# An eight-period pipelined kernel (Mamba, MoE, LSTM attention, MoE) on one core: TensorE gets matmuls whose result nobody reads in slots that hold no wide one

## What is computed

```python
x = layernorm(x + mamba(x))          # conv, 16 states a channel, a linear scan over time
x = layernorm(x + moe16(x))          # 16 experts, top 2, and one shared expert
x = layernorm(x + lstm_attention(x)) # LSTM of width 20, then a Gaussian position attention
x = layernorm(x + moe4(x))           # 4 layers of 4 experts, top 2

def step(carry, xg_t):               # the LSTM, 1024 steps one after the other
    h, c = carry
    i, f, gg, o = split(xg_t + h @ W_hh.T, 4)
    c = sigmoid(f) * c + sigmoid(i) * tanh(gg)
    h = sigmoid(o) * tanh(c)
```

## Time and profile before

| | |
|---|---|
| median of 3 runs | 3135.28 us (3131.15 to 3146.74) |
| the profiled execution | 3143.73 us |
| its span, first to last instruction | 3141.7 us |
| mean granted TensorE clock | 0.803 |
| first period (LSTM steps 0 to 127) | 327.6 to 646.2 us |
| attention slots 4 to `att` of periods 1 to 7 | 312 us together |
| LSTM's last step | ends at 2934.8 us |

### The profile page before, as it was taken

One profiled execution on the slowest core, in us unless ns is written; L12 is line 12 of the kernel. 1 busy time (PEld: TensorE's weight loads), 2 busy tenths in 40 slices (PEclk: granted clock), 3 DMA queues, 4 the chain that ended last, 5 costly groups with the idle time before them and its releaser, 6 DMA issues.

```text
span 3141.7 us, 30770 instructions
## 1 busy us (share of the span) xinstructions
PE 2537.0 (81%) x7208; PEld 1271.2 (40%) x7208; DVE 1943.4 (62%) x6569; ACT 1386.7 (44%) x4620; POOL 1062.8 (34%) x913
## 2 busy tenths in 40 slices
PE   4776884479996989789886998788978997889598
PEld 1122443244444444344444443444444444444344
DVE  4857587357775777567766677577766555444422
ACT  3232433435544555445544554445534444444233
POOL 4735257104542445235432455244422001100200
PEclk7587655659996899878996899789978996788699
DMA  3231332003321233113220332122311220111021
GB/s 108 68 84 54 89 99 72 25 13 100 101 66 28 80 96 90 42 46 101 78 71 27 92 97 75 25 73 84 92 33 46 65 64 21 34 64 58 10 81 57
DMA packets 111774, 204.70 MB, mean 65 GB/s; under 512 B 14799, under 2 KB 24422, under 8 KB 111592
## 3 DMA queue, kind: packets, MB, share of 16 engines
q1 hardware_dynamic: 111592, 202.75, 22.1%
HBM read 195.36 MB, written 7.34 MB: 65 GB/s over the span
## 4 chain that ended last, share of the span: by engine, by line
PE 41%; DVE 28%; ACT 14%; issue 7%; POOL 1%; DVEq 0%; POOLq 0%; ACTq 0%
PE p_hid L656 8%; DVE state L1197 7%; PE p_turn L905 7%; PE p_misc L666 4%; ACT cell_t L919 4%; DVE cell L935 3%; DVE add_c L932 3%; PE p_acc L666 3%; DVE weighed L1206 2%; DVE p_turn L929 2%; PE p_misc L354 2%; PE p_gate L465 2%; DVE hist L940 2%; PE p_turn L475 1%; ACT cand L916 1%
## 5 line engine op out<-in xcount | busy, mean ns | idle before, releaser
L905 PEld LDWEIGHTS p_turn<-hist,w_hh 22*128 22x128 f32 x2048 | 371.6, 225 | 1148.2 <-DVE hist L940 1013.9
L905 PE MATMUL p_turn<-hist,w_hh 22*128 22x4 f32 x2048 | 457.3, 291 | 420.2 <-DVE hist L940 402.2
L656 PE MATMUL p_hid<-xhat,w 128*128 128x512 f32 x1024 | 581.8, 652 | 1.1 <-ACT hid L714 0.7
L919 ACT ACTIVATE cell_t<-cell 20x4 f32<-20x4 f32 x1024 | 207.7, 203 | 701.7 <-DVE cell L935 701.7
L1135 POOL TENSOR_TENSOR drive<-du,rows 128x512 f32<-128x512 f32 x256 | 473.4, 1849 | 63.2 <-DVE state L1197 44.9
L929 DVE SCALAR_TENSOR_TENSOR p_turn<-p_turn,cell 20x4 f32<-20x4 f32 x1024 | 170.7, 167 | 500.8 <-ACT p_turn L915 478.9
L714 ACT ACTIVATE hid<-p_hid,b1f 128x512 f32<-128x512 f32 x512 | 351.6, 687 | 243.1 <-PE p_misc L666 151.1
L388 POOL TENSOR_TENSOR n_rstd<-n_var,minus_half 128x4 f32<-128x4 f32 x56 | 62.0, 1108 | 1098.3 <-DVE n_var L376 1098.3
L1197 DVE TENSOR_TENSOR_SCAN state<-decay,drive 128x512 f32<-128x512 f32 x256 | 398.1, 1555 | 25.2 <-POOL drive L1139 15.7
L1154 POOL TENSOR_TENSOR y<-y,weighed 128x512 f32<-128x512 f32 x192 | 242.4, 1262 | 450.5 <-DVE weighed L1206 449.9
L940 DVE SCALAR_TENSOR_TENSOR hist<-p_turn,cell_t 20x4 f32<-20x4 f32 x1024 | 162.7, 159 | 275.6 <-ACT cell_t L919 275.6
(11 more groups left out here) (204 smaller groups left out, 3161.5 us busy)
## 6 DMA issues: line engine op xcount, KB each, us to landing
rows<-rows_dram SPq DMA_DIRECT2D x128, 512.0 KB, 5.0
w<-w_dram SPq DMA_DIRECT2D x128, 256.0 KB, 2.7
w<-in_w2T SPq DMA_DIRECT2D x128, 256.0 KB, 2.7
comb_b<-comb_dram SPq DMA_DIRECT2D x64, 512.0 KB, 4.7
rows<-comb_dram SPq DMA_DIRECT2D x128, 128.0 KB, 2.9
w<-in_w1T SPq DMA_DIRECT2D x16, 256.0 KB, 2.8
w_dram<-w SPq DMA_DIRECT2D x16, 256.0 KB, 2.4
out_xT<-result SPq DMA_DIRECT2D x8, 256.0 KB, 2.5
```

Source lines behind the costliest of these rows:

```text
L656: nc.tensor.matmul(p_hid[:, v % 2, :], w1[:, v // FB, (v % FB) * P:(v % FB + 1) * P], xhat[:, :], start=True, stop=True).then_inc(g_h, 1)
L905: nc.tensor.matmul(gate_bank(i)[:, :, t:t + 1], w_hh[:, :], before, start=False, stop=False, skip_group_check=True).then_inc(gates_done, 1)
L919: nc.scalar.activation(cell_t[64:64 + PE_, :], cell[32:32 + PE_, :], ACT.Tanh, scale=0.5).then_inc(cell_tanh, 1)
```

## The change

A function `fill_pe` multiplies `mean_w` (a constant 128x128 matrix) with columns of `w_gate` (expert weights that lie in SBUF) into a PSUM bank that holds nothing at that time. `filling` decides for each slot of the periods 0 to 7 whether one is issued, how wide (512 columns, or 256 where `layer0` has a wide matmul in that slot) and into which bank. It is called on TensorE's program alone, last in the slot:

```diff
+    def fill_pe(bank, columns):
+        nc.tensor.matmul(bank[:, 0:columns], mean_w[:, :], w_gate[:, 0:FB, :].rearrange("p u c -> p (u c)")[:, 0:columns],
+                         start=True, stop=True)
+
+    L0_WIDE = {1, 5, 7, 49, 51} | set(range(11, 46))
+
+    def filling(i, slot, o, k0, with0, pre_done, has_pre):
+        wide0 = 1 if with0 and k0 in L0_WIDE else 0
+        if i == 0:
+            if pre_done == 0 or pre_done > 10:
+                return p_hid[:, 1, :], CT >> wide0
+            return None, 0
+        q = i - 1
+        att, tail = att_slots(q), att_slots(q) + L * LAYER
+        if 4 <= slot < att:
+            wide1 = 1 if 8 <= slot < 8 + q or slot == 10 + q else 0
+            bank = p_acc1 if slot < 8 else p_hid[:, 1, :]
+            return (bank, CT >> wide0) if not wide1 else (None, 0)
+        if slot >= tail + 5 and (pre_done > 10 or not has_pre):
+            return p_hid[:, 1, :], CT
+        return None, 0
...
-            if layer0 and not (heavy and slot < CH) and slot >= (L0_AT if layer1 else 0):
+            with0 = bool(layer0) and not (heavy and slot < CH) and slot >= (L0_AT if layer1 else 0)
+            if with0:
                 next(layer0, None)
+                k0 += 1
...
+            if fill and slot < CH and i < NCH:
+                bank, columns = filling(i, slot, o, k0 - 1, with0, done["pre"], u + 1 < NCH)
+                if columns:
+                    fill(bank, columns)
```

More of the change, by code:

```diff
@@ L1428, in period @@
         slot = 0
+        fill, k0 = of.get("fill"), 0
         def advance(g, what, n):
@@ L1573, in start @@
                 pe.wait_ge(prep_v, 3)
-            of = dict(pre=mamba_pre_pe, scan=mamba_scan_pe, leave=mamba_leave_pe, fold=fold_pe, layer0=layer0_pe, layer1=layer1_pe, lstm=lstm_pe)
+            of = dict(pre=mamba_pre_pe, scan=mamba_scan_pe, leave=mamba_leave_pe, fold=fold_pe, layer0=layer0_pe, layer1=layer1_pe, lstm=lstm_pe,
+                      fill=fill_pe)
             whole(dict(of, start=start))
```

## The result

| | before | after |
|---|---|---|
| median of the timed runs | 3135.22 us (3131.15 to 3146.74) | 3159.77 us (3158.19 to 3161.61) |
| the profiled execution | 3143.73 us | 3161.61 us |
| its span | 3141.7 us | 3158.6 us |
| mean granted TensorE clock | 0.803 | 0.852 |

What follows compares the result with a forecast made beforehand. No one engine was taken to bound the kernel; the LSTM step chain sets the pace. Gains of 21, 20, 8 and 4 sum to 53 us, less 5 for clock falls: 48 off the 3135.28 us median, 3087 us, range 3060 to 3112.

Steps and rivals of the forecast that it cites:

- rival A: Whole kernel slower because the fills run at the low clock: about 3236 us; chance 0.08.
- Price of a cold fill in a bare step: Low-clock slot with nothing else in the way: a fill makes 1.83 us into about 2.4, 0.55 lost.
- First period, -21 us: First period: 55 bare steps give 10 us, expert matmuls 7, late starts 4, preparing 1.5, less 1.5 for the cold start.
- The folding (-7): First period, 383.4 to 481.8 us: expert matmul steps shorten from 4.0 to 2.6 us at full clock; 7 us gained.
- term 1: The first period's 21 us gain; called wrong if the folding's steps keep their length while the clock is full.
- Attention, -20 us: Attention, seven stretches: bare steps give 8 us, late starts 16, shorter L905 3, less 7 for cold starts and collisions.
- rival B: No change: VectorE's scans and attention's element-wise chain set the steps, collisions take two per period, 15 us; 3126 us; chance 0.12.
- The layers' first slots, -8: First slots of the layers start at full speed: about 4 us in the first period with layers, 1 in the others.
- Ends, -4 net: Periods' ends: 31 bare steps give 5.5 us, less three cold starts of 0.55; 4 us net gained.
- Slots 0 to 3, 0: Start of each period, not filled: L590's 22-row matmuls stay at clock 0.50, so nothing counted for 28 steps.
- C: The clock flickers, at full speed for two thirds of the filled time: half of the gain, 3112 us; chance 0.12.
- D: More gain than forecast: late starts go nearly whole and faster preparation lets scans begin sooner; 3055 us; chance 0.10.

Runs made afterwards that it cites:

- e7_clear: Changed kernel without the 35 fills in slots of L347, L456, L612 or L1284 (224 fills left): 3125.04 us, ratio 0.9965 to the kernel before.
- e4_rows22: Changed kernel with all 259 fills multiplying 22 rows in place of 128, same columns: 3261.7 us, ratio 1.0363 to the kernel before.
- e5_early: Changed kernel with each fill directly behind the slot's LSTM matmul, not last in the slot (255 fills): 3141.37 us, ratio 1.0022 to the kernel before.
- e8_chosen: Changed kernel cut to 56 fills: first period from slot 97 (two in slot 97) and ends of the last three periods; 3131.43 us, ratio 0.9988.
- e11_single: The kernel of e8_chosen with one fill in slot 97 instead of two, all else equal: 3132.93 us in its one run.
- the parts: Three kernels, each with only the changed kernel's fills of the first period, attention or periods' ends: ratios 1.0019, 0.9973 and 0.9980 to the kernel before.
- e10_combined_early: Changed kernel with 152 fills directly behind the LSTM matmul: first period from slot 97, attention without L347, L456, L612, fewer at ends; 3123.36 us, 0.9954.

## Why the prediction was wrong

**The step that failed** is "So I expect full speed after the first two or three slots of a filled stretch, and 0.9 or more in it". The filled stretches show 0.69, 0.75, 0.75 and 0.88 in the first period, 0.64 to 0.85 in attention, 0.73 to 0.89 at the ends. "Two or three slots" was only somewhat short: after a wait the clock was full again within three filled steps in the folding (376.71 to 387.29) and after five behind slot 97 (602.27 to 614.80). What failed is that it stays full. Of the eleven waits of TensorE of more than 2 us in the filled stretches, nine (both of 3.3 us, and seven of the nine of 2.2 to 2.8) began at the full clock and ended at the low one, so the steps behind them are cold. The prediction took 5 us off for this. The runs show 98 of 258 filled steps (38%) low in both kernels, at 0.40 us each, 39 us, against a gain of 16 in the 158 full ones: a smaller form of rival A. The prediction's own break-even ("at half of the filled time gain and loss are about even") does not follow from its own prices: at 0.55 lost and 0.18 gained, three in four must be warm, and three fifths were.

Step by step:

- *Bounds and chain.* Right: the step is 1.83 us at the low clock and 1.62 at the full one, 0.2 us won (0.18 said).
- *Price of a cold fill in a bare step.* 0.55 said, 0.69 measured (2.52 us). The fill starts 0.5 us after L905, as said, but the next L905 follows 2.01 us behind its start (602.78 to 604.79), not the 1.86 of the earlier trace rows.
- *First period, -21 us.* It came as +9.4. The bare steps were right where the clock held: 1.62 us from slot 103 on. They were counted too high, though: by the trace of the kernel before, 45 steps of the first period and 21 of attention last 1.78 to 1.87 us, where the prediction has 55 and 46. The folding (-7) was wrong in its second half: steps of 2.70 at the full clock came as worked out (2.6), but those that begin after a wait last 5.08 where 4.0 stood before, and the rest did not shorten: without the fills behind L1284, at a clock of 0.77, the stretch takes 98.2 us, and 98.4 before. That was named in the prediction as the sign that term 1 is wrong.
- *Attention, -20 us.* It came as +7.2. The gain from late starts is there where the clock is full: in period 1 the step of L606 and L447 took 4.0 us from L905 to L905 and takes 2.2 (the first rows below); from L606's start, as in the earlier trace rows, it is 3.5 and 1.9. But one collision per period at 0.7 was too few and too cheap: the step behind L347 alone costs 1.2 to 1.9 us in each of periods 2 to 6, from `hist` to `hist`, 8.6 us together, more than the whole loss of attention; with the fill left out there it is gone (`e7_clear`: 2.05 us in period 3). Attention as a whole still took 2.8 us more than before in `e7_clear`, at its other fills. This was in part rival B's collision, in size about its 15 us.

```profile
678.03 0.38 PE L905 MATMUL p_turn<-hist,w_hh 22*128 22x4 f32 x2
...
680.23 0.38 PE L905 MATMUL p_turn<-hist,w_hh 22*128 22x4 f32 x2
```

```profile
687.85 0.60 PE L456 MATMUL p_up<-ident,comb 128*16 128x128 f32 x4 [1.27 <-DVE comb L428]
688.29 1.02 PE L1410 MATMUL p_hid<-w_gate,mean_w 128*128 128x512 f32 x2
689.25 0.38 PE L905 MATMUL p_turn<-hist,w_hh 22*128 22x4 f32 x2
```

The second of these is the collision that the prediction took from the earlier trace rows: L905 0.96 us behind the fill's start, as said.
- *The layers' first slots, -8.* -1.5 in the layers' stretches as a whole, and +5.9 in the last norm; the layers move by more than this from build to build, so the term can't be told.
- *Ends, -4 net.* +3.5: where the clock held, steps of 1.62 (before 1.83), but five of the seven ends start cold and the other two fall to the low clock after their first fill.
- *Slots 0 to 3, 0.* Nearly right: 70.7 to 67.9 us. Above all in periods 1, 6 and 7 part of them ran at the full clock (means of 0.75, 0.73 and 0.60), which the prediction had not foreseen; the fills behind them all start at the low one, as it said.
- *The rivals.* A holds in two fifths of the fills, B's collisions in attention; C had the flicker, but at its gain (3112) it priced only the part at the full clock and not what the rest costs. D did not come. The mistake of the forecast, which C shares: the fill was priced by its mean clock, when its price is that of the clock it is issued at, and this is low after waits.

Shown by the runs: the price of a low-clock fill (`e4_rows22`), that placement behind TensorE's own work costs (`e7_clear`, `e5_early`), that a wait decides the clock of the steps behind it (`e8_chosen` against `e11_single`). By the classing of steps the loss is in the cold filled steps, in both profiled executions of the changed kernel (+39.4 and +37.2 us). Open: why the parts do not add (0.997 against 1.006). The layers, which hold no fill, take from 1621 to 1646 us in the builds with 128-row fills, and no run shows what decides it, so gains of a few us in the whole kernel, those of `e7_clear` to `e10_combined_early` too, may be only in part the fills' own.

## What to carry to other kernels

Work that is added only to hold TensorE's clock is paid at the clock at which it runs: 0.69 us for a 128x512 float32 fill in a short step that begins cold, against 0.21 gained in one that begins warm, so more than three in four filled steps must be warm. Put it inside waits of a few us that are there anyway, enough to span them, as in slot 97, and not between weight loads and the chain that sets the pace, as behind L347. Count the waits in a stretch before counting on a clock in it.

## What the runs showed of the hardware

TensorE at 98% busy with 22-row matmuls stays at 0.50, and such work lets a full clock fall. The slots 0 to 3 after the first period, on the changed kernel:

```profile
655.64 1.09 PE L590 MATMUL p_hid<-hist,w_mub 22*128 22x512 f32 x2
...
657.24 1.10 PE L590 MATMUL p_hid<-hist,w_mub 22*128 22x512 f32 x2
...
658.96 1.98 PE L590 MATMUL p_hid<-hist,w_mub 22*128 22x512 f32 x2
```

The first two take 1.1 us, the third 1.98. In the step of L347 shown above the clock was full at L905 (0.38) and low for the fill behind the eight weight loads with one column each. And a build that changes nothing in a stretch can shift it by 6 us of 240, with the granted clock at 0.96 and 0.92 (period 5's layers above).
